# Two attention layers and a spline layer, rescheduled from side-by-side halves to a pipeline of half-batches

## The reference

```python
x = x + attention_0(layernorm(x), ctx)     # 16 heads of 16, keys and values from ctx (77 rows), biases
x = x + spline_ffn(layernorm(x))           # layer 0's feed-forward part
x = x + attention_1(layernorm(x), ctx)     # one key/value head shared by all 16 heads, causal mask
# spline_ffn(xf):
cluster_gates = calibrate(xf @ cluster_sigs.T)            # 8 clusters
cluster = argmax(cluster_gates)
local = argmax(calibrate(xf @ sigs.T) within the cluster) # 8 of 64 tiles
comp = tanh(gelu(xf @ w1 + b1) @ w2 + b2)                 # 2 numbers per token
mag = relu(comp * spline_w1[tile] + b1[tile]) . spline_w2[tile] + b2[tile]
y = layernorm(xf + mag * directions[tile] * scale) * gamma + beta
# calibrate(v): i = sigmoid(v / temperature) * 7; linear interpolation between 8 knots
```

## Time and profile before

| | us |
|---|---|
| median of 3 runs (lowest, highest) | 3180.27 (3178.08, 3189.95) |
| the profiled execution | 3176.69 |
| its span, first to last instruction | 3174.9 |
| PE / PEld / DVE / ACT / POOL busy | 2438.9 / 1995.9 / 2016.0 / 1390.1 / 735.1 |
| mean granted TensorE clock | 0.889 |

### The profile page before, as it was taken

One profiled execution on the slowest core, in us unless ns is written; L12 is line 12 of the kernel. 1 busy time (PEld: TensorE's weight loads), 2 busy tenths in 40 slices (PEclk: granted clock), 3 DMA queues, 4 the chain that ended last, 5 costly groups with the idle time before them and its releaser, 6 DMA issues. The chain is left out here.

```text
span 3174.9 us, 43537 instructions
## 1 busy us (share of the span) xinstructions
PE 2438.9 (77%) x16502; PEld 1995.9 (63%) x16502; DVE 2016.0 (63%) x4679; ACT 1390.1 (44%) x2383; POOL 735.1 (23%) x639
## 2 busy tenths in 40 slices
PE   0747747757665899999985899999999567777775
PEld 0535525435435788888874899999999545454544
DVE  1776776776674466666653566565665456776867
ACT  0413424423334465555542444444444245454433
POOL 0213302312222224444434000000000363424020
PEclk9968868868777999999997999999999788899887
DMA  8200000000001000110001434343433321111000
GB/s 299 108 0 15 15 0 29 1 0 29 1 1 42 1 16 28 41 41 29 22 18 38 150 110 146 110 144 112 131 125 118 117 78 46 54 37 54 1 14 14
DMA packets 153951, 185.43 MB, mean 58 GB/s; under 512 B 21864, under 2 KB 119429, under 8 KB 153736
## 3 DMA queue, kind: packets, MB, share of 16 engines
q1 hardware_dynamic: 141448, 155.41, 14.9%
q0 software_dynamic: 12288, 27.15, 2.7%
HBM read 117.51 MB, written 71.43 MB: 60 GB/s over the span
## 5 line engine op out<-in xcount | busy, mean ns | idle before, releaser
L2095 POOL DMA_INDIRECT picked<-expert_out,so x128 | 126.6, 989 | 868.6 <-DMA so<-slots 764.7
L204 PE MATMUL SC<-Xhi,Whi 128*128 128x320 f32 x1024 | 320.2, 313 | 7.1 <-DVE Wlo L1888 5.3
L204 PE MATMUL SC<-Xlo,Whi 128*128 128x320 f32 x1024 | 317.3, 310 | 0.0
L204 PE MATMUL SC<-Xhi,Wlo 128*128 128x320 f32 x1024 | 317.2, 310 | 0.0
L1124 POOL TENSOR_TENSOR ff_Hlo<-ff_HF,ff_Hhi 128x512 fp32r<-128x512 f32 x112 | 147.9, 1321 | 417.0 <-ACT ff_Hhi L1257 416.9
L328 POOL TENSOR_TENSOR PR<-PR,rs 128x616 f32<-128x616 f32 x128 | 153.6, 1225 | 324.0 <-DVE rs L294 324.0
L204 PEld LDWEIGHTS SC<-Xhi,Whi 128*128 128x128 f32 x1024 | 193.3, 189 | 7.8 <-DVE Wlo L1888 5.7
L204 PEld LDWEIGHTS SC<-Xlo,Whi 128*128 128x128 f32 x1024 | 193.3, 189 | 0.0
L204 PEld LDWEIGHTS SC<-Xhi,Wlo 128*128 128x128 f32 x1024 | 193.1, 189 | 0.0
L1907 DVE TENSOR_TENSOR Hlo<-HF,Hhi 128x320 fp32r<-128x320 f32 x256 | 125.4, 490 | 104.2 <-ACT Hhi L1865 104.2
L1888 DVE TENSOR_TENSOR Wlo<-Wraw,Whi 128x1024 fp32r<-128x1024 f32 x96 | 114.6, 1223 | 119.2 <-ACT Whi L1853 119.2
(11 more groups left out here) (451 smaller groups left out, 6881.3 us busy)
## 6 DMA issues: line engine op xcount, KB each, us to landing
expert_in<-zeros SPq DMA_DIRECT2D x4, 5120.0 KB, 32.2
rowsin<-expert_in SPq DMA_DIRECT2D x32, 640.0 KB, 6.0
expert_out<-rowsout SPq DMA_DIRECT2D x32, 640.0 KB, 4.0
Wraw<-L_wg SPq DMA_DIRECT2D x32, 512.0 KB, 7.0
Wraw<-L_wu SPq DMA_DIRECT2D x32, 512.0 KB, 7.1
Wraw<-L_wd SPq DMA_DIRECT2D x32, 512.0 KB, 7.8
Xin<-x SPq DMA_DIRECT2D x10, 512.0 KB, 4.7
x_after_l_attention<-X SPq DMA_DIRECT2D x8, 512.0 KB, 2.8
```

Source lines behind the costliest of these rows:

```text
L204: last = nc.tensor.matmul(out, lhs[l], rhs[r], start=start and n == 0, stop=stop and n == 2)
L2095: nc.gpsimd.indirect_dma_start(picked[g][:, t, k, :], None, oute[:, :], bass.IndirectOffsetOnAxis(ap=so[g][:, t, k:k + 1], axis=0)).then_i ...
```

## The change

The loop over batch elements is gone. The eight half-batches (NH) run through one straight program in periods of 16 slots, h = -1 to 10. In period h the first eight slots hold the units of half h's layer 0 attention and the last eight those of half h - 2's layer 1 attention, one unit in a slot. `UNIT_AT` maps a slot to its unit. Beside the units each slot may hold other work, listed by slot in the loops: layer norm, keys, values and queries of half p = h + 1; output projection and norm of half h; the spline layer of half c1 = h - 1; norm and queries for layer 1 of half c2 = h - 2; the last output projection and the store of half c3 = h - 3. On TensorE a slot is: transpositions of the unit two slots back, scores of the next unit, values of the unit two slots back, then the rest. 

The four PSUM buffers are now given to roles and not to halves: `pscores`, `ptrans`, `mid`, `wide`. There are five X buffers, four `PR` buffers, and one of most others. Applying a layer norm (`apply`, L171 before) and the copies of the context are on ScalarE; the block-diagonal keys and values and the addition of the spline layer's output to X are on GpSimd; gamma is multiplied in one operation on VectorE. The table is looked up in two parts, 66 spline columns and 256 direction columns, each by 8 matmuls a half, and read from PSUM with no copy. `calibrate` has 8 operations in place of 13, on one half (32 columns). Sqrt stands in slots 0, 8, 10, 13; Gelu in slot 0; Tanh in slot 3. The removed stage bodies and merely renamed helpers are left out below.

```diff
+NXA = 5
+NPA = LAG + 2
+PERIOD = 2 * UNITS
+
+
+def attention_units():
+
+    units, at, after = [], {}, {}
+    for h in range(NH + 2):
+        for layer, half in ((0, h), (1, h - 2)):
+            if 0 <= half < NH:
+                for u in range(UNITS):
+                    at[(h + 1) * PERIOD + layer * UNITS + u] = len(units)
+                    units.append((layer, half, u))
+                after[layer, half] = len(units)
+    return units, at, after
+
+
+UNIT, UNIT_AT, AFTER = attention_units()
...
+            pscores, ptrans, mid, wide = SC[0], GP[0], GP[1], SC[1]
...
+                    for h in range(-1, NH + 3):
+                        p, c1, c2 = h + 1, h - 1, h - 2
+                        for s in range(PERIOD):
+                            n = UNIT_AT.get((h + 1) * PERIOD + s - 1)
+                            if n is not None:
+                                normalise(n)
+                            if s == 2 and 0 <= c2 < NH:
+                                add_row(c2, bo1r, xn_c, bias1_added)
+                            if s == 3 and 0 <= c2 < NH and c2 % G == 0:
+                                keys_and_values1(c2 // G)
+                            if s == 10 and p < NH and p % G == 0:
+                                keys0(p // G)
+                            if s == 10 and p < NH:
+                                add_row(p, bo0r, xn_p, bias0_added)
+                            if s == 12 and p < NH and p % G == 0:
+                                values0(p // G)
+                            if s == 14 and 0 <= c1 < NH:
+                                add_spline(c1)
+                            if s == 15 and 0 <= h < NH:
+                                add_row(h, betar, xn_a, beta_added)
...
+                    def apply(h, ready, dst, src, L, done):
+                        act.wait_ge(ready, h + 1)
+                        for t in range(TT):
+                            last = nc.scalar.activation(dst[:, t, :], src[:, t, :], ACT.Identity, bias=L["nm"][:, t:t + 1], scale=L["rstd"][:, t:t + 1])
+                        last.then_inc(done, 1)
...
+                    for h in range(-1, NH + 3):
+                        p, c1, c2 = h + 1, h - 1, h - 2
+                        for s in range(PERIOD):
+                            i = (h + 1) * PERIOD + s
+                            now, mixed = UNIT_AT.get(i), UNIT_AT.get(i - LAG)
+                            if mixed is not None:
+                                take_pt(mixed)
+                            if s == 0 and 0 <= c2 < NH:
+                                root(c2, var_c, LN["c"]["mv"], LN["c"]["sd"], sd_c)
+                            if s == 3 and 0 <= c1 < NH:
+                                local_exp(c1)
+                            if s == 8 and p < NH:
+                                root(p, var_p, LN["p"]["mv"], LN["p"]["sd"], sd_p)
+                            if s == 10 and 0 <= c1 < NH:
+                                root(c1, var_g, LN["g"]["mv"], LN["g"]["sd"], sd_g)
+                            if s == 13 and 0 <= h < NH:
+                                root(h, var_a, LN["a"]["mv"], LN["a"]["sd"], sd_a)
+                            if now is not None:
+                                exponentials(now)
+                            if mixed is not None:
+                                take_ot(mixed)
+                            if s == 0 and 0 <= c1 < NH:
+                                take_sig(c1)
+                                take_hidden(c1)
+                            if s == 1 and 0 <= c2 < NH:
+                                apply(c2, rstd_c, XN[c2 % G], X[c2 % NXA], LN["c"], xn_c)
+                            if s == 2 and 0 <= c2 < NH:
+                                take_xt(c2, xt_c_psum, xt_c)
+                            if s == 3 and 0 <= c2 < NH:
+                                take_q(c2, 1, q1_psum, bq1c, q1_ready)
+                            if s == 3 and 0 <= c1 < NH:
+                                tanh(c1)
+                            if s == 5 and 0 <= c1 < NH:
+                                take_one_hot(c1)
+                            if s == 6 and p < NH and p % G == 0:
+                                replicate(p // G)
+                            if s == 8 and p < NH and p % G == 0:
+                                take_keys(p // G)
+                            if s == 9 and p < NH:
+                                apply(p, rstd_p, XP, X[p % NXA], LN["p"], xn_p)
+                            if s == 11 and 0 <= c1 < NH:
+                                apply(c1, rstd_g, XN[c1 % G], XN[c1 % G], LN["g"], xn_g)
+                            if s == 12 and p < NH:
+                                take_xt(p, xt_p_psum, xt_p)
+                            if s == 13 and p < NH:
+                                take_q(p, 0, q0_psum, bq0c, q0_ready)
+                            if s == 14 and 0 <= h < NH:
+                                apply(h, rstd_a, XN[h % G], X[h % NXA], LN["a"], xn_a)
+                            if s == 15 and 0 <= h < NH:
+                                take_xt(h, xt_a_psum, xt_a)
+
...
+                    def look_up(h):
+                        pe.wait_ge(oh_ready, h + 1)
+                        for outs, cols, done in ((small, slice(D, D + SMALL), small_psum), (dirs, slice(0, D), dir_psum)):
                             for t in range(TT):
...
+                    for h in range(-1, NH + 3):
+                        p, c1, c2, c3 = h + 1, h - 1, h - 2, h - 3
+                        for s in range(PERIOD):
+                            i = (h + 1) * PERIOD + s
+                            following, mixed = UNIT_AT.get(i + 1), UNIT_AT.get(i - LAG)
+                            if mixed is not None:
+                                unit_transposes(mixed)
+                            if following is not None:
+                                unit_scores(following)
+                            if mixed is not None:
+                                unit_values(mixed)
+                            if s == 0 and 0 <= c1 < NH:
+                                pe.wait_ge(xt_a, c1 + 1)
+                                if h % G == 0 and h // G < B:
+                                    pe.wait_ge(v_taken, h // G + 1)
+                                if c1:
+                                    pe.wait_ge(dir_taken, c1)
+                                signatures(c1)
+                                compress(c1)
+                            if s == 1 and 0 <= c1 < NH:
+                                components(c1)
+                            if s == 2 and 0 <= c2 < NH:
+                                if c1 < NH:
+                                    pe.wait_ge(xt_a, c1 + 1)
+                                transposes(XN[c2 % G], c2, xn_c, xt_c_psum)
+                            if s == 3 and 0 <= c2 < NH:
+                                project_q(wq1, c2, xt_c, q1_psum)
+                            if s == 4 and 0 <= c3 < NH:
+                                pe.wait_ge(q1_ready, min(c2 + 1, NH))
+                                project_out(mid, 1, wo1, c3, y1_psum)
+                            if s == 5 and 0 <= c1 < NH:
+                                one_hot(c1)
+                            if s == 6 and 0 <= c1 < NH:
+                                if c3 >= 0:
+                                    pe.wait_ge(x_done, c3 + 1)
+                                elif c2 >= 0:
+                                    pe.wait_ge(q1_ready, c2 + 1)
                                 else:
...
+                                    pe.wait_ge(xt_a, c1 + 1)
+                                pe.wait_ge(comp_sum, c1 + 1)
+                                look_up(c1)
+                            if s == 8 and p < NH and p % G == 0:
+                                if c1 >= 0:
+                                    pe.wait_ge(small_taken, c1 + 1)
+                                keys(p // G)
+                            if s == 9 and p < NH and p % G == 0:
+                                if c1 >= 0:
+                                    pe.wait_ge(dir_taken, c1 + 1)
+                                values(p // G)
+                            if s == 10 and 0 <= h < NH:
+                                if p < NH and p % G == 0:
+                                    pe.wait_ge(kcol_ready, p // G + 1)
+                                    pe.wait_ge(v4_taken, 2 * (p // G + 1))
+                                elif c1 >= 0:
+                                    pe.wait_ge(small_taken, c1 + 1)
+                                project_out(mid, 0, wo0, h, y0_psum)
+                            if s == 12 and p < NH:
+                                if h >= 0:
+                                    pe.wait_ge(y0_taken, h + 1)
+                                else:
+                                    pe.wait_ge(kcol_ready, 1)
+                                    pe.wait_ge(v4_taken, 2)
```

(103 more changed lines are left out.)

723 lines of the change are left out of this document (365 added, 358 removed).

## The result

The changed kernel takes 3072.01 us (median of 4; 3068.88 to 3075.3) against 3182.97 for the kernel before on the same chip: ratio 0.965, 95% interval 0.9626 to 0.9674. That is 3.5% faster. The forecast was 3042 (0.958 of the profiled execution of the kernel before), range 2965 to 3125. The profiled execution has a span of 3073.6 us. In a second measurement of the same kernel the ratio was 0.9632 (0.9608 to 0.9657).

What follows compares the result with a forecast made beforehand. Bound: a chain with one engine active at a time, VectorE nearly the bound in attention. Six full periods (528 us) plus ends (223) make 751 against 886.4 us: 135 less, 3042 us, range 2965 to 3125.

Steps and rivals of the forecast that it cites:

- Bare slot: Slot holding only attention-unit work: 2.72 us, from a VectorE, GpSimd and TensorE loop of 5.4 us over two slots.
- Full period: 16 slots with all added work: 79 us of slot intervals plus surcharges of 4 and 5, 88 us.
- the walk: Slot-by-slot reckoning of intervals between shift ends, each set by VectorE, TensorE or ScalarE's chain; sum 79 us a period.
- The port's surcharge: VectorE operations with two SBUF operands lose time beside GpSimd: 4 us a period, bounds 0 and 15.
- The clock's surcharge: TensorE's granted clock below full level in full periods: 5 us a period, bounds 0 and 12.
- Table switches: ScalarE's Sqrt and Gelu loads in slots 0, 8, 10, 13: ten of 1.28 us a period.
- The ends: Start 18, period 0 41, period 1 64, period 8 52, period 9 38, drain 10: sum 223 us.
- A: Rival: VectorE alone bounds full periods, skew absorbs all imbalance; 90 us less, 2952 us; chance 0.12.
- B: Rival: port cost at its upper bound, each two-input VectorE operation waits; 11 us more in 8 periods, 3130; chance 0.10.
- C: Rival: uncovered table loads in slots 0, 8, 10 and 13 stretch the slots; 3105 us; chance 0.09.
- D: Rival: slots' extras run serially through in-order queues and one mid bank; 138 us a period, 3342 us; chance 0.12.
- E: Rival: no gain, as much idle time left as before, 111 us a period; chance 0.02.

Runs made afterwards that it cites:

- the move alone: Changed kernel with GpSimd's row additions and block-diagonal keys and values moved to slots 5, 6 and 11; ratio 0.9557 to the kernel before.
- the fillers: Changed kernel plus an unread 128 x 512 matmul in each slot without a unit in periods 0, 1, 8 and 9; ratio 0.9623 to the kernel before.

## Why the prediction was right, and where it was off

- **What bounds the kernel** (chains with one engine at work): right. The loop written out gave nothing, the work fell by 33 us on VectorE, and the time by 106 in the stretch.
- **Bare slot, 2.72 us**: nearly right (2.9 in the mean of the six bare slots of period 0).
- **Full period, 88 us**: 86.1 over periods 2 to 6, right in the sum, but partly by luck. Slots 0+1, 3, 4, 12, 13, 14 and 15 are within 0.6 us of the walk, which has no surcharge in it. Slots 5, 7, 9 and 11 are 1.1 to 1.6 us longer and slot 8 is 1.2 shorter. Furthest off are slot 2 (5.3, measured 7.7) and slot 10 (5.6, 7.9): both hold a row added on GpSimd behind the normalisation.
- **The port's surcharge, 4 us a period**: too small for the slots, and hidden in the sum. Lengthened operations cost about 7 us a period; the move alone won 4. The range of 0 to 15 held it. The Trainium skill (GPSIMD Engine Reference, "Key points") names contention for operations with two SBUF inputs; the trace agrees, with 209 and 1757 ns for the same operation, and it shows the form: the operation doesn't run slower, it waits until GpSimd's instruction ends.
- **The clock's surcharge, 5 us a period**: it looks too large. The granted clock of full periods is 0.85 to 0.87, above the 0.78 before, and 86.1 less the 7 us of lengthened operations is the 79 us of the walk at full clock, which leaves no room for 5 more (an estimate; no run took the clock's part of a period by itself). So the two surcharges missed in opposite directions.
- **Table switches**: their number was nearly right (9 to 11 loads in a full period, 71 in all, none for Tanh), their weight wrong. I let them set slot 8 at 5.4; without roots it is still 5.2. Of the drain that the Trainium skill (ScalarE: Activation LUTs, "What ACT_TABLE_LOAD costs") counts on top of a load the trace shows nothing, and 54 loads less changed the time by 11 us at most.
- **The number of full periods**: six were counted, but period 7 brings in no new half. With its last slot taken as the mean 5.3 it lasts 78 us; periods 2 to 7 are 508 us together where the forecast had 528. 8 of these 20 us come from period 7, the rest from the shorter period; both hid a part of the error in the ends.
- **The ends, 223 us: the step that failed.** They measure 272. Start to the first shift 24 (18 forecast to the scores 2.5 earlier), period 0 48 (41), period 1 73 (64), from period 8 to the end 126 (100). The 49 us missing here and the 20 us too many in the full periods make the 29 by which the stretch of 780 us exceeds the forecast's 751.

  Each end is a row of dependent steps, and two things in it were mispriced. First the clock: I priced the steps at full clock, whereas from period 0 on TensorE had 0.64 to 0.84 of it there (a projection 6.04 us and not 3.6). Where two executions show the same stretch of program at two clocks, this comes to 16 us: 7.5 in the pause before period 2, and with the fillers 3.4, 2.4 and 0.9 in three other pauses and 1.8 among the units of period 9. It is an estimate and a lower bound, since the fillers also stand in the way and the clock stayed below full in places.

  Second the chain and the queue: at full clock the pause before period 9 still lasts 26 us, where I had 16 and the 4 of a light slot. The last two units need 10 us until their outputs are copied (791.4 to 801.8), and ScalarE applies the norm only behind them; and an output projection stands between the queries and the next unit's scores:
```profile
814.36 3.72 PE L823 MATMUL GP<-wo,OT 128*128 128x256 f32 x16 [1.36 <-ACT QT L696]
818.01 0.79 PE L176 MATMUL SC<-Kbd,QT 64*128 64x308 f32 x4
```
  Before period 2 keys and values stand in front of a unit's transpositions: GpSimd has normalised the unit at 191.98 us, and they start behind TensorE's value products:
```profile
198.72 2.05 PE L872 MATMUL GP<-wv,crep 128*128 128x256 f32 x4
200.57 1.27 PE L854 MATMUL GP<-ident,PR 128*128 128x128 f32 x5
```
  How the rest divides between queue and dependent latencies wasn't tried.
- **Rivals.** A (VectorE alone the bound) didn't come: the period is 86.1 and not 73, and VectorE is idle 14% of the steady stretch. B's mechanism is real, at half its price. C fell. D and E didn't occur; D's period of 111 is not reached even with the scores last (95.9), though 80 of the 110 us hang on that order.

## What to carry to other kernels

When stages with one active engine are laid under a steady loop, price each slot as the largest of its engines with one slot of skew, then price the fill and drain as chains at the low clock, each step with what stands ahead of it in its queue: there the forecast failed. Put the operation that feeds the bounding engine's next slot ahead of all filler work in the feeding queue; here that was worth 80 us. Place GpSimd's long operations in slots in which VectorE reads PSUM or only reduces and takes statistics, and don't buy this by delaying what GpSimd itself must deliver. A single operand in SBUF isn't enough: the copies of the context waited for GpSimd too.

## What the runs showed of the hardware that was not expected

A VectorE operation of 32 columns with two SBUF operands waits for the end of GpSimd's running instruction, and the next one can be caught again by the instruction behind it: 1.19 and 2.28 us in a row where 0.19 each is their own time. A copy from SBUF to SBUF is held in the same way (0.23 us alone, up to 2.45 beside GpSimd). Not held beside GpSimd were reductions (0.78 to 0.80 us), the statistics of a norm (0.41) and operations with an operand in PSUM (L995, 0.80; L1083, 0.47).

ScalarE's table load cost its 1283 ns in all 71 cases. The loads of the stretch by line, with ScalarE's idle time before them at the end:
```profile
L702 ACT ACT_TABLE_LOAD x34 | 43.6, 1283 | 0.6
L681 ACT ACT_TABLE_LOAD x27 | 34.6, 1283 | 0.5
L739 ACT ACT_TABLE_LOAD x8 | 10.3, 1283 | 0.1
```
Behind 69 of the 71 loads the next activation starts after 12 ns; the other two wait for VectorE's shift. And 54 loads fewer gained at most 11 us.
